# First attention of a two-layer block: probabilities scaled before their transposes instead of outputs after the value matmuls

## The chip, the cores and the metric
The kernel runs on one core of a Trainium2 chip, as one program. The metric is the device time in microseconds of a whole execution, the median of several. The profile is of one further execution; its times are counted from the start of its span.

## The reference
`x` is 8 x 256 x 1024 and the context `ctx_4096` 8 x 256 x 1024, both float32. Two layers of gated attention and feed-forward follow one another. Only the attention of layer 0 is touched here:

```python
x = rmsnorm(layernorm(x), ln_w)
q = (x @ wq.T)                       # 32 heads of 32
k, v = ctx @ wk.T, ctx @ wv.T        # 8 heads of 32, each used by 4 query heads
scores = q @ k.T / sqrt(32)          # 256 x 256 for each of 8 x 32 heads
attn = softmax(scores, axis=-1)
out = (attn @ v) ... @ wo.T
x = x + tanh(g_xattn[0]) * out
```

Softmax is exp(s - max) divided by its row sum. The division can be done on the probabilities or, since the sum belongs to a query row, on the rows of `attn @ v`.

## The kernel before
The program is a row of stages, each a block in which the five engines run their own instruction lists and meet only by semaphores: context projections, attention 0 (`attn0_stage`), its output projection, the feed-forward of layer 0, attention 1 and the last matmul. Attention 0 is the stage from about 178 to 684 us.

In it the 8 batches are taken two per turn of a loop (three turns, and the last pair written out). A batch has 16 units, n = 0 to 15. A unit is one tile t = n // 2 of four heads, and one half qb = n % 2 of the 256 query rows. Step n of TensorE's list does, in this order: the eight transposes of the probabilities of unit n (line 941, four heads by two halves kt of the keys, into the two banks of `psT`); the four score matmuls of unit n+2 (line 931, into `psS`); the sixteen value matmuls of unit n-1 (line 954, into `psO`); and a piece of the next batch's query projection (steps 0 to 3: four transposes of x, line 890; step 4, 7, 10, 13: 24 matmuls; the others 12, line 906). In the last batch that place is taken by small matmuls for an update table (line 981). Behind the values of the second half of a tile stand two transposes (line 960) that turn the spread reciprocals into the layout of the outputs.

Softmax of unit n+2 in step n: VectorE takes the negated maximum of four heads (line 1038), ScalarE computes four exponentials with their sums (line 1115) into `prob`, which has two buffers, n % 2. ScalarE's step n is first the eviction of `psT` for unit n (line 1132), then these exponentials. In odd steps from 5 VectorE evicts the first bank instead (line 1078).

VectorE's step n is a list in this order: a split of the query or of the transposed x into high and low parts (lines 1031, 1033, where step n has one); the eviction of line 1078 (odd n from 5); in odd steps the reciprocal of a tile's eight sums (line 1083); the maximum of n+2; in even steps `normalise_o` of the tile before (lines 1046 and 1048: evict the transposed reciprocals, then multiply the values by them). Steps 6 and 9 also have statistics for the batch after next, step 12 its normalisation, which waits for GpSimd's `rstd_of` (lines 622 to 634). GpSimd's list has one copy per tile that spreads eight reciprocals over 256 columns (line 860), and `rstd_of` after the copy of tile 5.

Results of four tiles are stored by SyncE's queue (line 797), which also loads `q_stack` (line 789), the keys, the values and x.

```python
BANK0_DVE = set(range(XFILLS + 1, UNITS, 2))
COPY_STEP = {f + 1: f for f in range(XFILLS)}
for t in range(KT - 1):
    COPY_STEP[XFILLS + 1 + 3 * (t // 2) + 2 * (t % 2)] = XFILLS + t
```

Of the kernel before, what the change touches and what calls it, by code (L numbers as in the profile page):

```python
# [16 lines left out]
F32 = mybir.dt.float32  # L17
# [4 lines left out]
ALU = mybir.AluOpType  # L22
# [4 lines left out]
P = 128  # L27
B, S, D = 8, 256, 1024
TT = S // P
KT = D // P  # L30
PAIRS = B // 2
HD0, NH0, NKV0 = 32, 32, 8
# [3 lines left out]
JH0 = P // HD0  # L36
# [7 lines left out]
HALF_N = 512  # L44
# [15 lines left out]
def hold(engine, sh):  # L60

    engine.sem_inc(sh.held, 1)
# [624 lines left out]
def attn0_stage(nc, sh, c, scratch, wq, rows, norm):  # L687
# [11 lines left out]
    ident = sh.ident  # L699
    UNITS = KT * TT  # L700
# [9 lines left out]
    with ExitStack() as es:  # L710
        def sb(name, shape, dt=F32):
            return es.enter_context(nc.sbuf_tensor("a_" + name, shape, dt))

        def sem(name):
            return es.enter_context(nc.semaphore("a_" + name))
# [8 lines left out]
        v0 = sb("v0", [P, 2, TT, KV0])  # L724
        prob = sb("prob", [P, 2, JH0, S])
        probT = sb("probT", [P, 2, TT, JH0, P])
        negmax = sb("negmax", [P, 2, JH0])
        sums = sb("sums", [P, 2, TT, JH0])
        recip_head = sb("recip_head", [P, 2, TT, JH0])
        recip = sb("recip", [P, 2, TT, JH0, HD0])  # L730
        recipT = sb("recipT", [P, S])
        oT = sb("oT", [P, KT, S])
        psS = es.enter_context(nc.psum_tensor("a_psS", [P, 4, HALF_N], F32))
        psT = es.enter_context(nc.psum_tensor("a_psT", [P, 2, HALF_N], F32))
        psO = es.enter_context(nc.psum_tensor("a_psO", [P, 2, S], F32))
        psQ = es.enter_context(nc.psum_tensor("a_psQ", [P, HALF_N], F32))
        coefs = sb("coefs", [P, NE, KT, RR])
        masks = sb("masks", [P, NE, KT, RR], U8)
# [12 lines left out]
        scores_full, max_ready, exp_done = sem("scores_full"), sem("max_ready"), sem("exp_done")  # L751
        psT_full = [sem(f"psT_full{p}") for p in range(2)]
        psT_copied = [sem(f"psT_copied{p}") for p in range(2)]
        head_ready, recip_ready = sem("head_ready"), sem("recip_ready")
        psO_full, recipT_ready = sem("psO_full"), sem("recipT_ready")
        o_ready = sem("o_ready")
        o_stored = [sem(f"o_stored{h}") for h in range(2)]
        coefs_loaded = sem("coefs_loaded")
# [93 lines left out]

        @block.gpsimd
        def _(pool):
            def spread_reciprocals(b, t):


                pool.wait_ge(head_ready, KT * b + t + 1)
                hold(pool, sh)
                nc.gpsimd.tensor_copy(recip[:, t % 2], recip_head[:, t % 2].unsqueeze(3).broadcast_to([P, TT, JH0, HD0])  # L860
                                      ).then_inc(recip_ready, 1)

            def body(i, final):
                for u in range(2):
                    b = 2 * i + u
                    for t in range(KT):
                        spread_reciprocals(b, t)
                        if t == 5 and not final:
                            norm.rstd_of(pool, b + 2, rms=True)

            with pool.Fori(0, PAIRS - 1) as i:
                body(i, False)
            body(PAIRS - 1, True)

        @block.tensor
        def _(pe):
# [57 lines left out]
                last.then_inc(scores_full, 1)  # L934

            def transposes(b, n):
                pe.wait_ge(exp_done, UNITS * b + n + 1)
                for kt in range(TT):
                    pe.wait_ge(psT_copied[kt], UNITS * b + n + 1)
                    for j in range(JH0):  # L940
                        last = nc.tensor.transpose(psT[:, kt, j * P:(j + 1) * P],  # L941
                                                   prob[:, n % 2, j, kt * P:(kt + 1) * P], ident[:, :])
                    last.then_inc(psT_full[kt], 1)

            def values(b, u, n):
                t, qb = n // TT, n % TT
                if qb == 0:
                    pe.wait_ge(o_ready, KT * b + t + 1)
                for kt in range(TT):
                    pe.wait_ge(psT_copied[kt], UNITS * b + n + 2)  # L950
                for kt in range(TT):
                    for j in range(JH0):
                        head = (t // REP0) * JH0 + j
                        nc.tensor.matmul(psO[j * HD0:(j + 1) * HD0, 0, qb * P:(qb + 1) * P],
                                         v0[:, u, kt, head * HD0:(head + 1) * HD0], probT[:, n % 2, kt, j, :],
                                         start=(kt == 0), stop=(kt == TT - 1))
                if qb == TT - 1:
                    pe.wait_ge(recip_ready, KT * b + t + 1)
                    for s in range(TT):
                        last = nc.tensor.transpose(psO[:, 1, s * P:(s + 1) * P],  # L960
                                                   recip[:, t % 2, s, :, :].rearrange("p j c -> p (j c)"), ident[:, :])
                    last.then_inc(psO_full, 1)

            for f in range(XFILLS):
# [49 lines left out]
        def _(dve):  # L1014
# [20 lines left out]
            def maximum(b, n):  # L1035
                dve.wait_ge(scores_full, UNITS * b + n + 1)
                bank = 2 * (n % 2)
                nc.vector.tensor_reduce(negmax[:, n % 2, :], psS[:, bank:bank + 2, :].rearrange("p a (j k) -> p (a j) k", k=S),  # L1038
                                        AX_X, ALU.max, negate=True).then_inc(max_ready, 1)

            def normalise_o(b, t):

                if t % QUAD == 0:
                    dve.wait_ge(o_stored[t // QUAD], 16 * JH0 * b + 1)
                dve.wait_ge(psO_full, KT * b + t + 1)
                nc.vector.tensor_copy(recipT[:, :], psO[:, 1, :]).then_inc(recipT_ready, 1)
                dve.wait_ge(recipT_ready, KT * b + t + 1)
                nc.vector.tensor_tensor(oT[:, t, :], psO[:, 0, :], recipT[:, :], ALU.mult).then_inc(o_ready, 1)


            for use in range(Q_USES - 1):
                split(0, use, True)
            maximum(0, 0)
            maximum(0, 1)
            dve.wait_ge(coefs_loaded, 16 * 4 * NE)
            nc.vector.tensor_tensor(coefs[:, :, :, :], coefs[:, :, :, :], masks[:, :, :, :], ALU.mult).then_inc(masked_done, 1)
            dve.wait_ge(masked_done, 1)
# [4 lines left out]
            def copy_update(quarter):  # L1062
                dve.wait_ge(update_full, quarter + 1)
                nc.vector.tensor_scalar(update[:, quarter * QUARTER:(quarter + 1) * QUARTER], psQ[0:RR, 0:QUARTER], 0.5, None, ALU.mult
                                        ).then_inc(update_copied, 1)

            def body(i, final):
                for u in range(2):
                    b = 2 * i + u
                    more = not (final and u == 1)  # L1070
                    for n in range(UNITS):
                        if n == 0:
                            split(b, Q_USES - 1)
                        elif n in COPY_STEP and more:
                            split(b + 1, COPY_STEP[n])
                        if n in BANK0_DVE:
                            dve.wait_ge(psT_full[0], UNITS * b + n + 1)
                            nc.vector.tensor_copy(probT[:, n % 2, 0, :, :],
                                                  psT[:, 0, :].rearrange("p (j q) -> p j q", j=JH0)).then_inc(psT_copied[0], 1)
                        if n % 2:  # L1080
                            t = n // 2
                            dve.wait_ge(exp_done, UNITS * b + n + 1)
                            nc.vector.reciprocal(recip_head[:, t % 2], sums[:, t % 2]).then_inc(head_ready, 1)  # L1083
                        if n + 2 < UNITS:
                            maximum(b, n + 2)
                        elif more:
                            maximum(b + 1, n + 2 - UNITS)
                        if n and n % 2 == 0:
                            normalise_o(b, n // 2 - 1)

                        if n == 6 and not final:
                            dve.wait_ge(x_loaded[u], 16 * i + 16)
                            norm.stats_of(x[:, u], 0)
                        if n == 9 and not final:
                            norm.moments_of(dve, b + 2, x[:, u], last_tile_only=True)
                        if n == 12 and not final:
                            norm.normalise(dve, b + 2, x[:, u], x[:, u], norm.STEPS_RMS)
                        if n > UPDATE_STEP and (n - UPDATE_STEP) % 3 == 0 and not more:
                            copy_update((n - UPDATE_STEP) // 3 - 1)
                    normalise_o(b, KT - 1)  # L1100
                    if not more:
                        copy_update(3)

# [1392 lines left out]
```

## Time and profile before

| | us |
|---|---|
| median of 3 executions | 1555.8 (1555.3 to 1561.07) |
| the profiled execution, its own time | 1561.66 |
| its span | 1559.9 |
| busy: TensorE, VectorE, ScalarE, GpSimd | 1411.1, 993.5, 761.7, 429.0 |
| attention 0: first and last transposes of probabilities | 182.2 and 680.9 |

In the rows below a line number is followed by the engine (PE TensorE, PEld its weight loads, DVE VectorE, ACT ScalarE, POOL GpSimd), the operation, what it writes and reads, and its shape. The `a_` names are those of attention 0. Times of single instructions are read to some 0.05 us, since their ends overlap with the next one's start.

### The profile page before, as it was taken

To read this page: it belongs to the slowest core of one execution; us is meant where nothing else is said; L and a number is where in the kernel's file an instruction comes from. 1 tells how busy PE (TensorE), PEld (TensorE's weight loads), DVE (VectorE), ACT (ScalarE), POOL (GpSimd) and SP (SyncE) were. 2 spreads that over 40 slices of the span, in tenths; PEclk is the share of its full clock that TensorE was granted. 3 is DMA by queue.
4 is the path that set the end of the run, shared out by engine and by line. 5 is a ranking of instruction groups with operands and counts; after the bars stand their busy time and mean duration, and the time that the engine had idled before them with its cause. 6 is when DMAs were issued, how large, how long until landed. Compare 5 with 4: busy or idle time off the path is not lost. (4 is left out here: it accounts for less than half of the span.)

```text
span 1559.9 us, 29677 instructions
## 1 busy us (share of the span) xinstructions
PE 1411.1 (90%) x10918; PEld 1142.4 (73%) x10926; DVE 993.5 (64%) x1578; ACT 761.7 (49%) x1911; POOL 429.0 (28%) x467
## 2 busy tenths in 40 slices
PE   7997799999999999879999939999959999999478
PEld 6997798888988889657787728888736666666244
DVE  4362377677666776543323227787547999998687
ACT  4320277677666776742212101221127777777387
POOL 0010000101101010000101003243348888888324
PEclk9998899999999999989999969999979999999889
DMA  6643555365553652844554342200032222221013
GB/s 234 215 166 82 91 136 144 82 143 119 133 130 83 154 130 70 217 151 157 189 177 147 121 162 82 81 15 26 1 81 69 68 62 61 61 61 42 1 80 137
DMA packets 134277, 169.98 MB, mean 109 GB/s; under 512 B 28933, under 2 KB 106565, under 8 KB 134166
## 3 DMA queue, kind: packets, MB, share of 16 engines
q1 hardware_dynamic: 134166, 168.41, 38.4%
q8 instruction: 80, 1.31, 0.4%
q14 instruction: 31, 0.25, 0.1%
HBM read 84.84 MB, written 33.19 MB: 76 GB/s over the span
## 5 line engine op out<-in xcount | busy, mean ns | idle before, releaser
L1115 ACT ACTIVATE a_prob<-a_psS,a_negmax 128x256 f32<-128x256 f32 x512 | 237.0, 485 | 158.8 <-DVE a_negmax L1038 158.5
L1038 DVE TENSOR_REDUCE a_negmax<-a_psS 128x4 f32<-128x1024 f32 x128 | 154.4, 1207 | 70.8 <-PE a_psS L931 68.7
L860 POOL COPY a_recip<-a_recip_head 128x256 f32<-128x256 f32 x64 | 25.6, 400 | 531.7 <-DVE a_recip_head L1083 531.7
L941 PE MATMUL a_psT<-ident,a_prob 128*128 128x128 f32 x1024 | 137.5, 278 | 14.4 <-issue 6.0
L906 PE MATMUL a_psQ<-a_xT_hi,wq_hi 128*128 128x256 f32 x456 | 135.5, 297 | 0.4
L941 PEld LDWEIGHTS a_psT<-ident,a_prob 128*128 128x128 f32 x1024 | 116.4, 143 | 23.5 <-issue 12.6
L1132 ACT COPY a_probT<-a_psT 128x512 f32<-128x512 f32 x208 | 115.8, 609 | 34.5 <-PE a_psT L941 33.5
L906 PE MATMUL a_psQ<-a_xT_lo,wq_hi 128*128 128x256 f32 x456 | 127.8, 280 | 0.0
L906 PE MATMUL a_psQ<-a_xT_hi,wq_lo 128*128 128x256 f32 x456 | 127.7, 280 | 0.0
L1115 ACT ACTIVATION_READ_ACCUMULATOR a_prob<-a_psS,a_negmax 128x1 f32 x512 | 110.3, 216 | 0.0
L1290 PE MATMUL p_psY<-p_w_hi,p_o_hi 128*128 128x512 f32 x256 | 103.7, 405 | 2.5 <-DVE p_o_lo L1318 2.5
L2143 ACT ACTIVATE b_prob<-b_prob 128x1024 f32<-128x1024 f32 x64 | 67.9, 1061 | 77.3 <-DVE b_prob L2017 77.3
L1525 PE MATMUL f_psY<-w_ffn_hi,f_xT_hi 128*128 128x512 f32 x256 | 102.9, 402 | 1.4 <-DVE f_xT_lo L1553 1.4
L1525 PE MATMUL f_psY<-w_ffn_lo,f_xT_hi 128*128 128x512 f32 x256 | 102.1, 399 | 0.0
L1525 PE MATMUL f_psY<-w_ffn_hi,f_xT_lo 128*128 128x512 f32 x256 | 102.0, 399 | 0.0
L1290 PE MATMUL p_psY<-p_w_lo,p_o_hi 128*128 128x512 f32 x256 | 100.3, 392 | 0.0
L1290 PE MATMUL p_psY<-p_w_hi,p_o_lo 128*128 128x512 f32 x256 | 100.3, 392 | 0.0
L1612 ACT CAST f_xT_hi<-f_psT 128x512 fp32r<-128x512 f32 x32 | 16.7, 599 | 170.1 <-PE f_psT L1507 170.1
L931 PE MATMUL a_psS<-a_k_stack,a_q_stack 128*128 128x256 f32 x512 | 93.4, 305 | 4.2 <-issue 3.0
L2011 DVE TENSOR_REDUCE b_maxes<-b_psS 128x16 f32<-128x1024 f32 x64 | 78.0, 1219 | 27.3 <-PE b_psS L1919 26.4
L906 PEld LDWEIGHTS a_psQ<-a_xT_hi,wq_hi 128*128 128x128 f32 x456 | 86.7, 190 | 9.1 <-issue 5.9
L906 PEld LDWEIGHTS a_psQ<-a_xT_hi,wq_lo 128*128 128x128 f32 x456 | 85.9, 188 | 0.0
(234 smaller groups left out, 3524.3 us busy)
## 6 DMA issues: line engine op xcount, KB each, us to landing
a_q_stack<-a_q_hi SPq DMA_DIRECT2D x128, 128.0 KB, 2.7
a_q_stack<-a_q_lo SPq DMA_DIRECT2D x128, 128.0 KB, 2.9
c_raw<-lay_ctxT SPq DMA_DIRECT2D x16, 512.0 KB, 4.9
rows<-in_x SPq DMA_DIRECT2D x8, 1024.0 KB, 5.8
scratch_o<-a_oT SPq DMA_DIRECT2D x64, 128.0 KB, 2.1
p_o_lo<-scratch_o SPq DMA_DIRECT2D x8, 1024.0 KB, 5.5
p_x<-in_x SPq DMA_DIRECT2D x8, 1024.0 KB, 7.6
scratch_x<-p_x SPq DMA_DIRECT2D x8, 1024.0 KB, 4.0
```

Of the source, the lines that this page charges most:

```text
L860: nc.gpsimd.tensor_copy(recip[:, t % 2], recip_head[:, t % 2].unsqueeze(3).broadcast_to([P, TT, JH0, HD0])).then_inc(recip_ready, 1)
L906: last = nc.tensor.matmul(bank[:, 0:S], w[:, kt, t * P:(t + 1) * P], a[:, kt, :], start=(kt == 0 and w is wq.hi and a is xT_hi), stop=(kt ...
L931: last = nc.tensor.matmul(psS[:, 2 * (n % 2) + j // 2, (j % 2) * S:(j % 2 + 1) * S], q_stack[:, t, j, qb * P:(qb + 1) * P], k_stack[:, u, ...
L941: last = nc.tensor.transpose(psT[:, kt, j * P:(j + 1) * P], prob[:, n % 2, j, kt * P:(kt + 1) * P], ident[:, :])
L1038: nc.vector.tensor_reduce(negmax[:, n % 2, :], psS[:, bank:bank + 2, :].rearrange("p a (j k) -> p (a j) k", k=S), AX_X, ALU.max, negate=Tr ...
L1115: last = nc.scalar.activation(prob[:, n % 2, j, :], psS[:, 2 * (n % 2) + j // 2, (j % 2) * S:(j % 2 + 1) * S], ACT.Exp, bias=negmax[:, n % ...
L1132: nc.scalar.copy(probT[:, n % 2, kt, :, :], psT[:, kt, :].rearrange("p (j q) -> p j q", j=JH0)).then_inc(psT_copied[kt], 1)
L1290: last = nc.tensor.matmul(psY[:, 2 * t + h, :], a[:, u, kt, t * P:(t + 1) * P], w[:, kt, h * HALF_N:(h + 1) * HALF_N], start=(kt == 0 and ...
L1525: last = nc.tensor.matmul(psY[:, 2 * t + h, :], a[:, u, kt, rows], w[:, kt, cols], start=(kt == 0 and a is xT_hi and w is w_ffn.hi), stop= ...
L1612: nc.scalar.copy(xT_hi[:, u, 2 * n:2 * n + 2, :].rearrange("p k n -> p (k n)"), psT[:, n, :]).then_inc(xhi_ready, 1)
L2011: nc.vector.tensor_reduce(maxes[:, n % 2, :], psS[:, n % 2, :].rearrange("p (h k) -> p h k", h=NH1), AX_X, ALU.max).then_inc(max_ready, 1)
L2143: nc.scalar.activation(prob[:, n % 2, :], prob[:, n % 2, :], ACT.Exp).then_inc(exp_done, 1)
```

## The change
`recip`, `recipT`, the transposes of line 960 and the copy of line 860 go. VectorE takes the reciprocal of one unit's four sums in each step, for unit n+1 in step n, ahead of the maximum. GpSimd multiplies the whole unit of `prob` (128 x 1024) by it, in place, and TensorE's transposes wait for that instead of for the exponentials. The outputs are evicted by a plain copy.

```diff
-            def spread_reciprocals(b, t):
-                pool.wait_ge(head_ready, KT * b + t + 1)
+            def scale_probabilities(b, n):
+                pool.wait_ge(head_ready, UNITS * b + n + 1)
                 hold(pool, sh)
-                nc.gpsimd.tensor_copy(recip[:, t % 2], recip_head[:, t % 2].unsqueeze(3).broadcast_to([P, TT, JH0, HD0])
-                                      ).then_inc(recip_ready, 1)
+                nc.gpsimd.tensor_tensor(prob[:, n % 2], prob[:, n % 2],
+                                        recip_head[:, n // TT % 2, n % TT].unsqueeze(2).broadcast_to([P, JH0, S]), ALU.mult
+                                        ).then_inc(prob_scaled, 1)
...
-                        spread_reciprocals(b, t)
+                        for qb in range(TT):
+                            scale_probabilities(b, TT * t + qb)
                         if t == 5 and not final:
                             norm.rstd_of(pool, b + 2, rms=True)
...
             def transposes(b, n):
-                pe.wait_ge(exp_done, UNITS * b + n + 1)
+                pe.wait_ge(prob_scaled, UNITS * b + n + 1)
...
                 if qb == TT - 1:
-                    pe.wait_ge(recip_ready, KT * b + t + 1)
-                    for s in range(TT):
-                        last = nc.tensor.transpose(psO[:, 1, s * P:(s + 1) * P],
-                                                   recip[:, t % 2, s, :, :].rearrange("p j c -> p (j c)"), ident[:, :])
                     last.then_inc(psO_full, 1)
...
-            def normalise_o(b, t):
+            def copy_o(b, t):
...
                 dve.wait_ge(psO_full, KT * b + t + 1)
-                nc.vector.tensor_copy(recipT[:, :], psO[:, 1, :]).then_inc(recipT_ready, 1)
-                dve.wait_ge(recipT_ready, KT * b + t + 1)
-                nc.vector.tensor_tensor(oT[:, t, :], psO[:, 0, :], recipT[:, :], ALU.mult).then_inc(o_ready, 1)
+                nc.vector.tensor_copy(oT[:, t, :], psO[:, 0:S]).then_inc(o_ready, 1)
+
+            def reciprocals(b, n):
+                dve.wait_ge(exp_done, UNITS * b + n + 1)
+                nc.vector.reciprocal(recip_head[:, n // TT % 2, n % TT], sums[:, n // TT % 2, n % TT]).then_inc(head_ready, 1)
...
             maximum(0, 0)
             maximum(0, 1)
+            reciprocals(0, 0)
...
-                        if n % 2:
-                            t = n // 2
-                            dve.wait_ge(exp_done, UNITS * b + n + 1)
-                            nc.vector.reciprocal(recip_head[:, t % 2], sums[:, t % 2]).then_inc(head_ready, 1)
+                        if n + 1 < UNITS:
+                            reciprocals(b, n + 1)
+                        elif more:
+                            reciprocals(b + 1, 0)
                         if n + 2 < UNITS:
                             maximum(b, n + 2)
```

## Rows read from the trace of the kernel before

**Rows 1.** The page, section 1: busy us, share of the span, instructions.
```profile
PE 1411.1 (90%) x10918; PEld 1142.4 (73%) x10926; DVE 993.5 (64%) x1578; ACT 761.7 (49%) x1911; POOL 429.0 (28%) x467
```
**Rows 2.** Busy time by stretch: length, engines, PE clock, DMA share, GB/s.
```profile
240.00:303.00 63.00, 61.96 (x690) 55.79 (x689) 45.47 (x79) 45.23 (x160) 5.62 (x15) 1.00 0.51 122
```
**Rows 3.** Waits in 178 to 625 us: total, times, longest.
```profile
PEld a_psT L941 <- ACT a_prob L1115: 6.5, 6, 3.0
```
**Rows 4.** Timeline of TensorE: start, length; starts of batches, one fifth unit, the last.
```profile
314.20 1.06 PE L941 MATMUL a_psT<-ident,a_prob 128*128 128x128 f32 x8 [3.01 <-issue]
...
325.18 1.06 PE L941 MATMUL a_psT<-ident,a_prob 128*128 128x128 f32 x8
...
375.18 1.04 PE L941 MATMUL a_psT<-ident,a_prob 128*128 128x128 f32 x8
...
439.46 1.94 PE L941 MATMUL a_psT<-ident,a_prob 128*128 128x128 f32 x8 [2.98 <-issue]
...
502.36 1.04 PE L941 MATMUL a_psT<-ident,a_prob 128*128 128x128 f32 x8
...
624.80 1.04 PE L941 MATMUL a_psT<-ident,a_prob 128*128 128x128 f32 x8
...
680.12 1.09 PE L941 MATMUL a_psT<-ident,a_prob 128*128 128x128 f32 x8
```
**Rows 5.** Timeline around one pair of reciprocal transposes.
```profile
304.87 0.44 PE L960 MATMUL a_psO<-ident,a_recip 128*128 128x128 f32 x2
...
305.06 0.36 PE L906 MATMUL a_psQ<-a_xT_hi,wq_hi 128*128 128x256 f32 x1
...
305.54 0.41 DVE L1046 COPY a_recipT<-a_psO 128x256 f32<-128x256 f32 x1
```
**Rows 6.** Timelines of VectorE, ScalarE and GpSimd: one unit's chain, then four reciprocals.
```profile
315.78 1.22 DVE L1038 TENSOR_REDUCE a_negmax<-a_psS 128x4 f32<-128x1024 f32 x1 [2.67 <-PE a_psS L931]
...
317.04 0.47 ACT L1115 ACTIVATE a_prob<-a_psS,a_negmax 128x256 f32<-128x256 f32 x1 [1.09 <-DVE a_negmax L1038]
...
318.75 0.21 ACT L1115 ACTIVATION_READ_ACCUMULATOR a_prob<-a_psS,a_negmax 128x1 f32 x1
...
318.24 0.19 DVE L1083 RECIPROCAL a_recip_head<-a_sums 128x8 f32<-128x8 f32 x1
...
318.60 0.40 POOL L860 COPY a_recip<-a_recip_head 128x256 f32<-128x256 f32 x1 [10.04 <-DVE a_recip_head L1083]
...
331.94 0.19 DVE L1083 RECIPROCAL a_recip_head<-a_sums 128x8 f32<-128x8 f32 x1
...
339.84 0.19 DVE L1083 RECIPROCAL a_recip_head<-a_sums 128x8 f32<-128x8 f32 x1
...
347.39 0.19 DVE L1083 RECIPROCAL a_recip_head<-a_sums 128x8 f32<-128x8 f32 x1
...
364.64 0.19 DVE L1083 RECIPROCAL a_recip_head<-a_sums 128x8 f32<-128x8 f32 x1
```
**Rows 7.** Timeline of GpSimd: the first and the last of the seven instructions of `rstd_of`.
```profile
357.12 0.22 POOL L622 TENSOR_SCALAR norm_tmp<-norm_moments 128x2 f32<-128x2 f32 x1
...
359.45 0.72 POOL L634 TENSOR_TENSOR norm_rstd<-norm_tmp,minus_half 128x2 f32<-128x2 f32 x1
```
**Rows 8.** Groups of GpSimd (busy, mean ns); then one line's min/median/max.
```profile
L1848 POOL TENSOR_TENSOR b_halves<-b_prob 128x512 f32<-128x512 f32 x64 | 82.9, 1296 | 6.5 <-ACT b_prob L2143 6.0
...
L860 POOL COPY a_recip<-a_recip_head 128x256 f32<-128x256 f32 x64 | 25.6, 400 | 531.7 <-DVE a_recip_head L1083 531.7
...
L1814 POOL TENSOR_TENSOR b_kbd<-b_group_mask,b_keys_lo 128x512 fp32r<-128x512 f32 x16 | 20.4, 1276 | 0.0
...
L1489 POOL TENSOR_TENSOR stream<-stream,f_bias x16: 2441/3008/3392, 943.3 to 1116.6; 128x1024 f32 x12, 128x1024 f32<-128x1024 f32 x4
```
**Rows 9.** Busy time by stretch, as rows 2: after a loop's jump, and with gaps.
```profile
439.00:441.00 2.00, 1.54 (x8) 1.57 (x9) 0.00 (x0) 0.42 (x1) 0.00 (x0) 0.50 0.83 210
...
630.00:634.00 4.00, 3.30 (x39) 2.78 (x39) 2.01 (x4) 4.00 (x15) 0.00 (x0) 1.00 1.04 280
```

## What the change is expected to do
> **What bounds the kernel now.** The page comes first: one core, a span of 1559.9 us, TensorE busy for 90% of it, VectorE 64%, GpSimd 28% [rows 1]. That share is a mean over stages, so the second view is the table of busy time by stretch. In the attention stage (units run from 182 to 684 us) a stretch of 63 us has TensorE busy for 61.96, VectorE 45.5, ScalarE 45.2 and GpSimd only 5.6 [rows 2]. TensorE is the bound there, and GpSimd is almost free; that much speaks for the change. The third view is the table of waits: over seven batches TensorE's weight loads wait for the exponentials only 6.5 us in all [rows 3]. So the softmax chain has slack, but this view does not say how much per unit. The fourth is the timeline, which does.
>
> I call t(n) the start of the transposes of unit n. On TensorE a batch of 16 units goes from t(0) = 314.20 to the next t(0) = 375.18, which is 60.98 us. The 17 starts, whose first, fifth and last stand in [rows 4], lie apart by 1.81, 3.58, 2.79, 2.80, 5.07, 3.54, 3.70, 4.95, 3.71, 3.53, 5.12, 3.53, 3.71, 4.98, 3.68 and 4.48 us, so the first four units take 10.98 together. Units are short at first because they carry four transposes of x and long later because they carry 12 or 24 matmuls of the next query.
>
> **What it removes.** Each second unit loses two transposes of the spread reciprocals: from their start at 304.87 to the next matmul at 305.06 is 0.19 us, and there are 64 such pairs [rows 5]. Worth 64 x 0.19 = 12 us where TensorE is the limit, nothing where it waits. VectorE loses an eviction of 0.41 us per tile [rows 5]; it has idle time in each unit, so I cost that at nothing. GpSimd loses 64 copies of 0.40 us, also nothing [rows 8].
>
> **What it adds, and where.** A reciprocal of 0.19 us on VectorE in each unit instead of each second (hidden by VectorE's idle 17 us in 63 [rows 2], apart from its place in the chain), and a two-input GpSimd multiply on 128x1024 between the exponentials and the transposes.
>
> **The price P of the multiply** is in no row of this stage. Nearest is the same shape in a later stage: 2.44 us at best, median 3.01; half that shape, 128x512, takes 1.296 on average beside a VectorE that mostly reads PSUM [rows 8], as it does here. Doubling 1.296 gives 2.6, but part of that is fixed. I take P = 2.5, next to the lowest whole-shape row, with ends of 1.0 (if a broadcast operand cost no reading; 128x256 with a broadcast copy takes 0.40 [rows 8], four times that is 1.6, less a fixed part) and 3.0 (the median, beside a VectorE on SBUF data). The Trainium skill (GPSIMD Engine Reference, section 3.1) puts a two-input elementwise operation at about 2.6 cycles per element at 1.2 GHz, which makes an estimate of 2.2 us here; by that the sum below would be about 18 us smaller. [...]
>
> **The chain over two units.** `prob` has two buffers, and the scores of unit n+2 are issued only after the transposes of n. Read off one unit [rows 4, 6]: transposes at 314.20, maximum starts 315.78 (1.58 later; I take 1.61, counted from the weight load), exponentials start 317.04 (1.26), last accumulator read ends 318.75 + 0.21 = 318.96 (1.92). New behind it: about 0.07 to the reciprocal, 0.36 from a reciprocal's start to GpSimd's (318.24 to 318.60), P, and 0.1 to TensorE; the two small gaps are estimates from the 0.04 to 0.1 that other hand-overs in these rows take. So t(n+2) is at least t(n) + 1.61 + 1.26 + 1.92 + 0.53 + P = t(n) + 5.3 + P, 7.8 us for a pair. Today the first two pairs take 10.98; they become 15.6.
>
> **The chain over one unit.** The reciprocal of unit n+1 now stands in VectorE's queue in step n, behind the split of the query and, in odd steps from 5, behind the eviction of psT, which waits for the transposes of n itself. Queued behind it is the maximum of n+2, for which ScalarE waits. From the reciprocal's start to TensorE is 0.36 + P + 0.1 = 2.96. Today's reciprocals in odd steps stand in that same place: step 5 at 331.94, 1.69 after its t; step 7 at 339.84, 2.35 after (two statistics are ahead of it); step 9 at 347.39, 1.24 after; step 13 at 364.64, 2.60 after (the row normalisation is ahead) [rows 6]; the four t, added up from the distances above, are 330.25, 337.49, 346.15 and 362.04. So these units take 4.65, 5.3, 4.2 and 5.55. Step 11 has another: the reciprocal square root follows scale 11 in GpSimd's queue, and runs from 357.12 to 359.45 + 0.72 = 360.17, 3.05 us [rows 7]; scale 12 is queued behind it: 3.05 + 2.5, less 0.1 of overlap with the start of step 11 and plus 0.1 to TensorE, is 5.55.
>
> **One batch**, in us, units in order: 0 to 3: 15.6; 4: 4.85; 5: 4.65; 6: 3.5; 7: 5.3; 8: 3.7; 9: 4.2; 10: 4.9; 11: 5.55; 12: 3.5; 13: 5.55; 14: 3.7; 15: 4.3. The units 4, 6, 10, 12 and 15 are TensorE's own time of today less 0.19. The sum is 69.3 against 60.98: 8.3 more. Seven batches have queries: 58. Less 3.5, since the seventh has no statistics and no rstd, and the fifth began at the slower clock and so was already longer: 62.90 from 439.46 to 502.36. The eighth has 55.3 us from its t(0) to its t(15) [rows 4]; seven pairs and a unit at the pair chain's 3.9 make 58.5, and the units with update matmuls stay above that in part: plus 4. The end loses an eviction of 0.41 and the pair of transposes: minus 0.5. Total plus 58. The loop's jump, about 3 us of TensorE every two batches, covers GpSimd's own jump and multiply (3 + 2.5), so nothing there.
>
> **Sum.** The profiled execution took 1561.66, which is 5.9 above the median of 1555.8. 1561.66 + 58 = 1620; against the median 1614. No DMA is moved; o and q transfers only get more time. About 0.5%, 8 us, is what a measurement of this kernel can tell from no change.
>
> **Rivals.**
> 1. *The multiply is cheap and hidden; not slower.* If P is near 1.0, a pair needs 6.3, the first four units 12.6 (1.6 more than today), every later unit goes back to TensorE's time, and seven removed pairs of transposes a batch give back 1.3. Net 0.3 a batch: 1558. For it: the second operand is one number per row. Against: of the two rows for 128x512, 1.276 has a broadcast operand (a mask repeated over a middle dimension) and 1.296 has none [rows 8]. Up to P = 1.5, one more us a batch, it would still not be told from no change; the gain would need P under about 0.9. Chance 0.07.
> 2. *Only the pair chain binds.* If splits and psT evictions run early enough, because TensorE is stalled and VectorE catches up, units 5 to 15 cost 7.8 per pair or their own time: 15.6 + 4.85 + 7.8 + 4.85 + 7.8 + 4.9 + 7.8 + 4.9 + 7.8 = 66.3, 5.3 a batch, plus 3 elsewhere: +40, 1596. Against: the odd-step eviction waits on t(n) whatever came before. Chance 0.18.
> 3. *Contention.* VectorE and GpSimd slow each other and P is 3.0. Eight steps of a batch hold P: 4 us a batch more, 32 in all: 1646. For it: the same shape ranges from 2.44 to 3.39 [rows 8]. Against: nearly all of VectorE's work here reads PSUM. The Trainium skill (GPSIMD Engine Reference, section 8) states contention only with VectorE instructions of two SBUF inputs or in a two-port mode; by that the rival stays small, and the trace agrees in that the 128x512 rows average 1.28 to 1.30. Chance 0.1.
> 4. *TensorE's clock falls.* In 439 to 441 us, just after 3 us of idle, the granted clock is 0.50 (1.2 GHz); in 630 to 634, with idle gaps of up to 2.1, it stays 1.00 (2.4 GHz) [rows 9]. The new gaps are under 2 us, except behind the loop's jump, where 2 us are added to 3. Today such a start cost the fifth batch 1.9 us (62.90 against 60.98). With a slow start in all batches, doubled by the further gaps: 8 x 3.8 = 30, 1644. Chance 0.1.
>
> **How the numbers follow.** The forecast has 0.55 and its own range of 1600 to 1630. The range reaches from under rival 2 and the smaller P (1588) to rivals 3 and 4 (1648). Faster 0.02 and same 0.05 come from rival 1 with P at its low end; slower is the rest, 0.93.
>
> **What would show it.** In the profile after: GpSimd busy in the stage some 128 x 2.5 = 320 us; TensorE's weight loads of the transposes waiting for GpSimd's write of `prob` by 80 us or more in all; a batch of 69 us, with 7.8 per pair in its first four units; scale 12 starting 3 us after scale 11 ended. Wrong if the multiply takes under 1.5 us, if TensorE still works through a batch in 61, or if the time after t(11) is that of unit 5.

## The result, and the profile after

The changed kernel takes 1579.6 us (median of 4) where the kernel before takes 1556.1 (median of 4). The medians lie 23.5 us apart; the recorded ratio of all fast runs is 1.0135, 95% interval 1.0115 to 1.0156, which is 21 us, and the text goes by the ratio. The forecast had the sign and the chain over two units, and more than twice the size: 1614, with a range that began at 1588.

First the page of the changed kernel, its busy times and the one row of GpSimd that is new (section 1; then the groups by line, columns as in [rows 8]), with what waited for it.

```profile
PE 1400.0 (89%) x10790; PEld 1128.0 (72%) x10798; DVE 979.3 (62%) x1578; ACT 761.0 (48%) x1911; POOL 645.8 (41%) x531
```
```profile
L856 POOL TENSOR_TENSOR a_prob<-a_prob,a_recip_head 128x1024 f32<-128x1024 f32 x128 | 242.4, 1893 | 333.9 <-DVE a_recip_head L1045 332.4 <-POOL norm_rstd L634 1.5
...
L939 PEld LDWEIGHTS a_psT<-ident,a_prob 128*128 128x128 f32 x1024 | 115.7, 144 | 66.0 <-POOL a_prob L856 55.2 <-issue 9.9
...
L1045 DVE RECIPROCAL a_recip_head<-a_sums 128x4 f32<-128x4 f32 x128 | 22.1, 172 | 61.2 <-ACT a_prob L1112 61.2
```

GpSimd is busy for 217 us more than in [rows 1], and the price P of the multiply is 1.893 us, with almost no spread. TensorE's weight loads of the transposes wait 55.2 us in all for it; in the kernel before they waited 6.5 us for the exponentials in a stretch of seven batches [rows 3]. The third row is a second wait that was not there: VectorE stands 61 us at the reciprocal, waiting for ScalarE, with the next maximum queued behind it.

The timeline of TensorE in the first units of the batch that begins at 387.22, which answers to [rows 4]:

```profile
387.22 1.09 PE L939 MATMUL a_psT<-ident,a_prob 128*128 128x128 f32 x8
...
390.78 1.09 PE L939 MATMUL a_psT<-ident,a_prob 128*128 128x128 f32 x8 [1.50 <-POOL a_prob L856]
...
394.35 1.09 PE L939 MATMUL a_psT<-ident,a_prob 128*128 128x128 f32 x8 [0.84 <-POOL a_prob L856]
...
397.91 1.09 PE L939 MATMUL a_psT<-ident,a_prob 128*128 128x128 f32 x8 [0.84 <-POOL a_prob L856]
...
401.47 1.09 PE L939 MATMUL a_psT<-ident,a_prob 128*128 128x128 f32 x8 [0.84 <-POOL a_prob L856]
```

The four units take 401.47 - 387.22 = 14.25 us, 7.13 a pair, where the forecast's formula 5.3 + P gives 7.2 for P = 1.89. From here on t(n) is read at the weight load of the first transpose, which moves single units by up to 0.1 us. The sixth batch, which has no loop jump in it, takes 63.67 us from t(0) to t(0), against 61.27 for the same batch before. Its units, in order: 3.56, 3.57, 3.56, 3.57, 4.82, 4.08, 3.47, 4.86, 3.50, 3.68, 4.82, 4.10, 3.46, 4.86, 3.50, 4.26. Units 0 to 3, 5, 9 and 11 are those in which the next transposes start right behind the multiply; the others are TensorE's own time and 0.09 to 0.3 shorter than before. The removed transposes account for most of that, not for all: units 7 and 13 had none.

Over the stage of the two profiled executions: t(0) of the first batch is 4.0 us later, the eight batches are 1.4, 2.5, 4.3, 2.6, 1.8, 2.4, 2.3 and 1.0 longer, and the end gives back 0.8: 21.4 us. Of the 4.0 the change made 2.3: from the first scores to t(0) 6.28 us pass instead of 3.98. The other 1.7 had passed before the first scores, where nothing of the change has run; over all twelve traces the first scores start anywhere from 178.2 to 180.9. So the stage itself costs 19.7 in this pair. The spans differ by 16.9 only, since 4.5 us less pass in the later stages of the changed kernel's execution; the profiled execution of the kernel before was itself 5.5 above its median.

### The profile page after: what moved, and what is told of

Same layout as the page of the kernel before. It is cut to its first block and busy times, and to the rows that moved or that the text cites. A ratio compares the mean times of both kernels' runs of the same rounds, so it can differ in the third digit from the quotient of the medians.

```text
span 1576.8 us, 29597 instructions
## 1 busy us (share of the span) xinstructions
PE 1400.0 (89%) x10790; PEld 1128.0 (72%) x10798; DVE 979.3 (62%) x1578; ACT 761.0 (48%) x1911; POOL 645.8 (41%) x531
## 5 line engine op out<-in xcount | busy, mean ns | idle before, releaser
L856 POOL TENSOR_TENSOR a_prob<-a_prob,a_recip_head 128x1024 f32<-128x1024 f32 x128 | 242.4, 1893 | 333.9 <-DVE a_recip_head L1045 332.4
L939 PEld LDWEIGHTS a_psT<-ident,a_prob 128*128 128x128 f32 x1024 | 115.7, 144 | 66.0 <-POOL a_prob L856 55.2
L1112 ACT ACTIVATION_READ_ACCUMULATOR a_prob<-a_psS,a_negmax 128x1 f32 x512 | 104.0, 203 | 0.0
L1360 POOL TENSOR_TENSOR w_ffn_lo<-p_full,w_ffn_hi 128x512 f32 x16 | 20.4, 1293 | 184.9 <-ACT w_ffn_hi L1397 184.9
```

The lines of the kernel that those rows point to most:

```text
L856: nc.gpsimd.tensor_tensor(prob[:, n % 2], prob[:, n % 2], recip_head[:, n // TT % 2, n % TT].unsqueeze(2).broadcast_to([P, JH0, S]), ALU.m ...
L939: last = nc.tensor.transpose(psT[:, kt, j * P:(j + 1) * P], prob[:, n % 2, j, kt * P:(kt + 1) * P], ident[:, :])
L1112: last = nc.scalar.activation(prob[:, n % 2, j, :], psS[:, 2 * (n % 2) + j // 2, (j % 2) * S:(j % 2 + 1) * S], ACT.Exp, bias=negmax[:, n % ...
```

## Experiments

Each is a small edit of the changed kernel or of the one named. Ratios are to the kernel before, run beside it on the same chip.

**1. The multiply nearly without its duration.** Only two of 256 columns of each head are scaled, so most of the normalisation is left out; every wait stays.

```diff
-nc.gpsimd.tensor_tensor(prob[:, n % 2], prob[:, n % 2],
+nc.gpsimd.tensor_tensor(prob[:, n % 2, :, 0:2], prob[:, n % 2, :, 0:2],
-    recip_head[...].unsqueeze(2).broadcast_to([P, JH0, S]), ALU.mult
+    recip_head[...].unsqueeze(2).broadcast_to([P, JH0, 2]), ALU.mult
```


> The changed kernel with the GpSimd multiply cut to 2 of the 256 key columns of each head (the other columns stay unscaled, so most of the normalisation is left out); every wait, the reciprocal of each unit and the plain eviction stay. Theory A (all of the 21 us comes from the multiply's duration P = 1.89 in the chain, and the removed transposes do pay): with P near 0.3 the pair chain is 5.5, the steps go back to TensorE's time, and the removed pairs of transposes are gained: 1546 to 1550. Rival B (the cost lies in VectorE's queue: the maximum now stands behind a reciprocal that waits for exponentials): still above 1560.

Measured 1549.4, ratio 0.9938 (0.9914 to 0.9962). The instruction takes 0.20 us. The rest of the change is worth 10 us, and the multiply's duration costs those and 21 more. Rival B falls as an account of the whole. It has a part, though: VectorE's timeline in the first units of the sixth batch of this run.

```profile
502.25 0.18 DVE L1045 RECIPROCAL a_recip_head<-a_sums 128x4 f32<-128x4 f32 x1 [0.68 <-ACT a_prob L1112]
502.34 1.23 DVE L1032 TENSOR_REDUCE a_negmax<-a_psS 128x4 f32<-128x1024 f32 x1
...
505.57 0.18 DVE L1045 RECIPROCAL a_recip_head<-a_sums 128x4 f32<-128x4 f32 x1 [0.68 <-ACT a_prob L1112]
```

The reciprocals are 3.32 us apart, and each waits for exponentials although the multiply costs next to nothing. That is a ring of its own: exponentials of n+1, 1.92, reciprocal and hand-overs 0.14, maximum of n+2 1.26, and then the exponentials of n+2. Units 2 and 3 take 3.33 each here and 2.80 before; the first four take 12.1 against 11.3. The forecast had the reciprocal's place in the queue, but not this ring.

Not all of the 10 us come from the removed transposes. The matmuls of the query start 0.118 us apart in the kernel before and 0.113 in the changed one, at the same granted clock and already ahead of the stage. These windows, of the kernel before and then of the changed one, count the matmuls of that line alone (length, TensorE, weight loads, clock, DMA share, GB/s).

```profile
160.00:174.00 14.00, 14.00 (x121) 14.00 (x120) 1.00 0.44 104
```
```profile
160.00:174.00 14.00, 14.00 (x125) 14.00 (x125) 1.00 0.33 79
```

Over the seven batches with queries the mean distance is 0.1168 before and 0.1143 in this run, which makes 3 us (an estimate, 1176 distances). Run 5 below has 0.118 ahead of the stage too, but so has run 9, and the other runs have 0.113: it goes neither with the multiply nor with the transposes, and its cause is open.

**2. A full operand.** The broadcast reciprocals are replaced by a tile of ones, so the normalisation is left out.

```diff
-nc.gpsimd.tensor_tensor(prob[:, n % 2], prob[:, n % 2],
-    recip_head[:, n // TT % 2, n % TT].unsqueeze(2).broadcast_to([P, JH0, S]), ALU.mult
+nc.gpsimd.tensor_tensor(prob[:, n % 2], prob[:, n % 2], unit[:, :, :], ALU.mult
```


> The changed kernel with the multiply by a full 128x1024 tile of ones in place of the broadcast reciprocals (the normalisation is left out). It asks where the forecast's P of 2.5 failed. Theory A1 (the broadcast of one number over 256 columns saves reading time): the multiply takes 2.44 to 2.5 and, by the forecast's chain with the rest as measured, a batch takes 67.9 instead of 63.7 and the whole 1610 to 1618. Rival A2 (two-input multiplies of this shape take 1.9 whatever the operand, and the 2.44 was contention): the multiply takes 1.9 and the time stays at 1579.

Measured 1606.1, ratio 1.0300 (1.0275 to 1.0326). This view is of the line's instructions, min/median/max in ns:

```profile
L858 POOL TENSOR_TENSOR a_prob<-a_prob,a_unit x128: 2340/2382/2407, 183.5 to 724.9; 128x1024 f32<-128x1024 f32 x128
```

The tile of ones is written once, ahead of the loop (not shown in the diff). A1 holds in kind: with a full second operand the same multiply takes 2.38 us, with one number for 256 columns 1.89. The time missed its expected 1610 to 1618 by 4 us; P is 2.38 and not 2.44 to 2.5, which at the price of the next sentence accounts for 3 to 6 us. Between these two kernels 0.49 us of P makes 26 us, 53 us per us.

**3. The multiply twice.** The probabilities are scaled by the squared reciprocal.

```diff
+nc.gpsimd.tensor_tensor(prob[:, n % 2], prob[:, n % 2], recip..., ALU.mult).then_inc(first_done, 1)
+pool.wait_ge(first_done, UNITS * b + n + 1)
 nc.gpsimd.tensor_tensor(prob[:, n % 2], prob[:, n % 2], recip..., ALU.mult).then_inc(prob_scaled, 1)
```


> The changed kernel with the multiply done twice in a row on the same unit, the second waiting for the first (the probabilities are scaled by the squared reciprocal). Theory A: P is 3.9 to 4.0, the first four units of a batch take 2 x (5.24 + 4.0) = 18.5 instead of 14.3, a batch about 80 to 84, the whole 1700 to 1750. Rival (GpSimd's part is mostly beside other work): below 1650.

Measured 1728.6, ratio 1.1101 (1.1067 to 1.1135): as theory A has it. The first four units of the sixth batch take 18.6 us, and a batch 82 to 86 (the last, without a query, 74). The rival, below 1650, falls.

```profile
607.39 0.86 PEld L944 LDWEIGHTS a_psT<-ident,a_prob 128*128 128x128 f32 x8 [1.55 <-POOL a_prob L861]
...
626.00 0.86 PEld L944 LDWEIGHTS a_psT<-ident,a_prob 128*128 128x128 f32 x8 [2.67 <-POOL a_prob L861]
```

The four kernels with P = 0.20, 1.89, 2.38 and 3.8 stand at -0.6%, +1.35%, +3.0% and +11.0%. One us of P costs 18 us on average between the first two, 53 and then 86: the more units of a batch are set by the multiply, the steeper. Between 0.20 and 1.89 nothing was run.

**4. Scores ahead of transposes.** If the pair chain holds the scores and the maximum because scores of n+2 stand behind the transposes of n in TensorE's list, then turning the two shortens it.

```diff
 for n in range(UNITS):
-    transposes(b, n)
+    pe.wait_ge(exp_done, UNITS * b + n + 1)
     if n + 2 < UNITS:
         scores(b, i, u, n + 2)
     elif more:
         scores(b + 1, i + u, 1 - u, n + 2 - UNITS)
+    transposes(b, n)
```


> The changed kernel with TensorE issuing the scores of unit n+2 ahead of the transposes of unit n, after a wait for the exponentials of n. Theory A: the pair chain no longer holds scores and maximum; what is left is exponentials 1.92, hand-over 0.43, multiply 1.89, 0.1, transposes and the eviction of their second bank about 1.7, which is 6.0; the first four units take about 12.1 instead of 14.3, the later steps stay as they are (VectorE's queue holds their reciprocals): about 1562, 1556 to 1568. Rival B (VectorE's queue sets the short steps): no change from 1579.

Measured 1561.3, ratio 1.0008 (0.9997 to 1.0020): nearly all of the 21 us gone, 18 by the medians and 20 by the ratios. Units 0 to 3 of the sixth batch take 3.08, 3.30, 3.32, 3.32, together 13.0 instead of 14.25. That is not the expected 12.1: what now ends last is the ring of experiment 1. The batch fell by more than its short units, 61.8 against 63.67, because unit 5 went from 4.08 to 3.64 and unit 11 from 4.10 to 3.90, which was not expected and is not explained here. So of 1.9 us a batch the pair chain accounts for the 1.2 of the first four units.

**5. The same order in the kernel before.**

```diff
-    transposes(b, n)
+    pe.wait_ge(exp_done, UNITS * b + n + 1)
     ...scores of n + 2...
+    transposes(b, n)
```


> The kernel before, with TensorE's scores of unit n+2 ahead of the transposes of unit n and nothing else. It asks whether the 18 us that this order took off the changed kernel belong to the multiply's chain. Theory A: here the steps are TensorE's own but for the first four of a batch, where at most 1.2 us lie above its work: 0 to 5 us faster, 1554 to 1560 against 1560. Rival: the order is worth the same 18 us anywhere (1542).

Ratio 0.9993 (0.9981 to 1.0006), 1559.0 against 1560.9. The order is worth nothing there that can be told, so the rival's 1542 falls: the 18 us are there only with the multiply in place.

**6. The reciprocal ahead of the eviction of psT**, on top of 4, in VectorE's odd steps from 5.

```diff
+    reciprocals(b, n + 1)        # in its three cases
     if n in BANK0_DVE:
         dve.wait_ge(psT_full[0], UNITS * b + n + 1)
         nc.vector.tensor_copy(probT[:, n % 2, 0, :, :], ...)
-    reciprocals(b, n + 1)
```


> scores_first with VectorE's reciprocal of unit n+1 ahead of its eviction of psT in the odd steps from 5. Theory (those steps wait for the multiply because the reciprocal stood behind an eviction that waits for this unit's transposes): steps 5, 9 and 11 go from 3.64, 3.64 and 3.90 to 3.50 to 3.55, 0.6 a batch: about 1557, 1555 to 1559. Rival: unchanged, 1561.

Ratio 0.9995 (0.9984 to 1.0006), 1560.1 against 1560.9. The time stays where the rival had it, and misses the expected 1555 to 1559. Units 5 and 9 do go to 3.49 as expected, so the place behind the eviction was what held them; at 0.15 each that is too little to tell in the whole. Unit 11 does not: it takes 3.97. GpSimd's timeline shows why.

```profile
421.24 0.22 POOL L622 TENSOR_SCALAR norm_tmp<-norm_moments 128x2 f32<-128x2 f32 x1
...
423.57 0.71 POOL L634 TENSOR_TENSOR norm_rstd<-norm_tmp,minus_half 128x2 f32<-128x2 f32 x1
424.53 1.90 POOL L856 TENSOR_TENSOR a_prob<-a_prob,a_recip_head 128x1024 f32<-128x1024 f32 x1 [0.26 <-POOL norm_rstd L634]
```

Here scale 12 waits for the end of `rstd_of`, which costs the unit half a microsecond (3.97 against 3.49).

**7. `rstd_of` two units later**, on top of 6, and the normalisation that needs it too.

```diff
-                        if t == 5 and not final:
+                        if t == 6 and not final:
                             norm.rstd_of(pool, b + 2, rms=True)
...
-                        if n == 12 and not final:
+                        if n == 14 and not final:
```


> recip_early with GpSimd's rstd_of moved from behind scale 11 to behind scale 13, and the normalisation that waits for it from step 12 to step 14 on VectorE. Theory: step 11 took 3.97 us against 3.49 for its neighbours because scale 12 stood behind 3 us of rstd_of; behind scale 13 the same 3 us lie beside the 4.85 us step 13: step 11 goes to 3.5, six batches, 3 us less: 1557 where the kernel before has 1560.9, a ratio of 0.997 to 0.999. Rival: it only moves the wait to step 13 or 14, ratio 0.9995 to 1.001.

Ratio 0.9982 (0.9968 to 0.9996), 1558.2 against 1560.4. Unit 11 takes 3.49 and unit 13 5.03 instead of 4.85. It came out as expected. Of the versions that keep the whole computation this is the only one whose interval lies under the kernel before, by 0.2%, and its end is 0.9996; that small gain is close to nothing. Against the changed kernel it is about 1.5% less.

**8. The maximum ahead of the reciprocal in the short steps**, on top of 6, to break the ring of experiment 1.

```diff
-                        reciprocals(b, n + 1)
+                        if n >= XFILLS:
+                            reciprocals(b, n + 1)
...
                         maximum(b, n + 2)
+                        if n < XFILLS:
+                            reciprocals(b, n + 1)
```


> recip_early, with the maximum ahead of the reciprocal in steps 0 to 3. Theory: the 3.3 us of a short step are a chain of its own, exponentials 1.92, reciprocal 0.14, maximum 1.26, since the maximum of n+2 stands behind the reciprocal of n+1 that waits for exponentials; with the order turned it goes, and the short steps fall to the 6.0 pair: 1 us a batch less, about 1549, 1547 to 1554, under both kernels. Rival: the later reciprocal gives it back, 1557.

The rival had the right direction and too small a size: 1573.8, ratio 1.0087 (1.0074 to 1.0101), where it said 1557. VectorE's timeline at the start of the fourth batch:

```profile
384.82 0.42 DVE L1028 TENSOR_TENSOR a_q_lo<-a_psQ,a_q_hi 128x256 fp32r<-128x256 f32 x1
385.16 1.21 DVE L1033 TENSOR_REDUCE a_negmax<-a_psS 128x4 f32<-128x1024 f32 x1
386.30 0.17 DVE L1046 RECIPROCAL a_recip_head<-a_sums 128x4 f32<-128x4 f32 x1
```

The exponentials of unit 1 were done at 384.6, so its reciprocal could have started at 385.16, when the split ended; it starts 1.14 later, behind a maximum, and the multiply and the transposes are late by as much. In the trace the first units of a batch take 4.2 and 4.6 at their longest. With the multiply in the chain the reciprocal is the more urgent of the two.

**9. The reciprocals on GpSimd**, on top of 7, so that VectorE's queue holds none.

```diff
-pool.wait_ge(head_ready, UNITS * b + n + 1)
+pool.wait_ge(exp_done, UNITS * b + n + 1)
+nc.gpsimd.tensor_tensor(recip_head[...], sums[...], unit[:, :], ALU.pow).then_inc(head_ready, 1)
+pool.wait_ge(head_ready, UNITS * b + n + 1)
```


> rstd_late with the reciprocals taken off VectorE: GpSimd raises the four sums to the power -1 itself, waits for it, and multiplies. It tells the two chains of a short step apart. If the 3.3 us of steps 1 to 3 are the chain over VectorE's queue (exponentials 1.92, reciprocal 0.14, maximum 1.26), they go although P grows by 0.8 to 1.1, and become the pair chain 6.0 - 0.36 + 0.9 = 6.5, or 3.25 a step, with odd and even steps unlike: no gain in sum, and the long steps stay at TensorE's time: ratio 0.998 to 1.001. If they were the pair chain over the multiply, they grow by 0.4 a step, 1.5 us a batch: ratio 1.004 to 1.01.

Ratio 1.0186 (1.0163 to 1.0209), outside both expectations. The power over 128x4 takes 1.01 us, so P is about 3.0 with the hand-over. The first four units take 14.0 against 13.0; the first expectation gives 13.0 and the second 14.6. Units 6, 12 and 13 grow too (4.25, 4.25, 6.25), which neither has. The run doesn't separate the two chains: both may have been at work in the kernel it was made from. Experiment 1 does, and the ring over VectorE rests on that.

**10. The multiply in two halves of the keys**, on the changed kernel alone.

```diff
+for kt in range(TT):
+    keys = slice(kt * P, (kt + 1) * P)
-    nc.gpsimd.tensor_tensor(prob[:, n % 2], prob[:, n % 2], ...
+    nc.gpsimd.tensor_tensor(prob[:, n % 2, :, keys], prob[:, n % 2, :, keys], ...
...
-                pe.wait_ge(prob_scaled, UNITS * b + n + 1)
                 for kt in range(TT):
+                    pe.wait_ge(prob_scaled, TT * (UNITS * b + n) + kt + 1)
```


> The changed kernel with the multiply in two instructions, by halves of the keys, each releasing its four transposes. Theory A: the half costs 1.0 to 1.05, so the second half ends 2.05 after the start and its four transposes 0.45 later, against 1.89 + 0.9: 0.3 a pair of units less, 8 a batch in the steps that wait: 1572 to 1578. Rival (a GpSimd instruction has a fixed cost that eats it): 1579 or more.

Measured 1573.4, ratio 1.0079 (1.0063 to 1.0094); a half takes 1.04 us, so both together 2.08 against 1.89.

```profile
L858 POOL TENSOR_TENSOR a_prob<-a_prob,a_recip_head x256: 1038/1040/1044, 183.1 to 693.2; 128x512 f32<-128x512 f32 x128
```

That is inside the expected 1572 to 1578. GpSimd is busy for longer and the kernel takes 6 us less than the changed one (9 by the ratios, whose intervals are apart): it is the latency to the transposes that counts, not GpSimd's load.

## Why the prediction was right in sign and wrong in size

- **What bounds the kernel, and that the multiply lands in a chain over two units: right.** 5.3 + P gives 7.2 a pair; 7.13 was measured. In runs 2 and 3 it gives 7.7 and 9.1, and the first pair of the sixth batch takes 7.6 and 9.1. Of the forecast's other signs, the size of each fell short with P: GpSimd's multiplies take 242 us and not 320, TensorE's weight loads wait 55 and not 80 or more, a batch takes 63.7 and not 69.
- **The step that failed is the price P**, "I take P = 2.5, next to the lowest whole-shape row". It is 1.893. The rows it came from all had two operands that change along the row; run 2 shows that this is the difference, 2.38 against 1.89. The mask with a broadcast over a middle dimension, 1.276 in [rows 8], was read as a sign that broadcasts save nothing. It repeats a row and not one number, which is another case. The copy of 128x256 at 0.40 from just such an operand was used for the lower end only. With P = 1.89 in the forecast's own table a batch comes to 65.2 instead of 69.3, and its sum to about +27 instead of +58. That is 1583, under the range too: the range began at 1588 although the forecast let P go down to 1.0.
- **Step 11: the wrong wait.** The forecast added the 3.05 us of `rstd_of` and a multiply from t(11) on, and named as a sign of being wrong that the unit takes as long as unit 5. It does: 4.10 against 4.08, where the table gives 4.94 at the right P. Scale 11 ends 1.09 us before t(11) = 562.20, since unit 10 is a long one of TensorE, so most of `rstd_of` lies in that time. What ends last is the reciprocal behind the eviction, as in unit 5; the rows are from the sixth batch, of VectorE and of GpSimd.

```profile
563.90 0.17 DVE L1045 RECIPROCAL a_recip_head<-a_sums 128x4 f32<-128x4 f32 x1
```
```profile
563.40 0.71 POOL L634 TENSOR_TENSOR norm_rstd<-norm_tmp,minus_half 128x2 f32<-128x2 f32 x1
564.36 1.89 POOL L856 TENSOR_TENSOR a_prob<-a_prob,a_recip_head 128x1024 f32<-128x1024 f32 x1 [0.25 <-POOL norm_rstd L634]
```

  Scale 12 starts 0.46 after its reciprocal, where other units have 0.35: `rstd_of` costs 0.1 here, and the half microsecond of run 6 only when the reciprocal comes earlier. Over six batches the step was 5 us too long.
- **What else stands between 27 and the stage's 19.7.** Units 8 and 14 kept 3.7 in the table, though they lose a pair of transposes as well (3.50 measured): 0.4 a batch too much. In the other direction the first batch was left out: the multiply also stands before its first transposes, 2.3 us that the forecast put at nothing. That the sum at the right P comes as near as 27 to 21 is in part luck of these terms.
- **A slip of counting.** By its own table seven multiplies a batch count, not the eight of rival 3, so its 32 us are 28, and the 18 us less by the Trainium skill's price are 16.
- **Steps 5, 9: right** (4.04 and 3.6 at that P, measured 4.08 and 3.68), and run 6 shows that the eviction ahead of the reciprocal was the reason. Steps 7 and 13, 4.7 and 4.95 by the chain, fell back to TensorE's 4.86.
- **Removed transposes: right in sign, the size not separated.** Run 1 is 10 us under the kernel before although it has the ring over VectorE, but some 3 us of that are the closer matmuls of the query. Units 7 and 13, which had no such transposes, are 0.09 and 0.14 shorter; units 4 and 10, as long and with a pair each, 0.26 and 0.29.
- **Missing from the forecast:** that ring, exponentials, reciprocal, maximum, 3.32 us a unit. It is hidden under the pair chain's 3.56 in the changed kernel, and is the next limit once that is shortened.
- **The loop's jump: nothing, as the forecast had it.** Unit 15 with the jump takes 7.54 and 7.51 us against 7.71 and 7.68 before. What differs is the start behind it: the third batch is 4.3 longer, where its neighbours are 2.5, and in it TensorE started at a granted clock of 0.50 (1.2 GHz) in the changed kernel's trace and of 1.00 (2.4 GHz) in the other's. These windows are of the two kernels, the first of the changed one: length, five busy times, and then the granted clock.

```profile
322.00:324.00 2.00, 1.97 (x10) 2.00 (x11) 0.00 (x0) 0.58 (x1) 0.43 (x1) 0.50 0.66 163
```
```profile
314.00:316.00 2.00, 1.80 (x16) 1.83 (x17) 0.22 (x1) 1.08 (x2) 0.00 (x0) 1.00 0.69 182
```

  The idle time before is 3.2 us in the changed kernel and 3.0 in the other, and the kernel before has such a slow start too, at 439 us, behind 3.0 us ([rows 4], [rows 9]). So one slow start more or less in a profile is not shown to be the change's doing. Rival 4 as a cost in each batch fell: in 387 to 454 us the clock is 1.00.
- **Rivals.** Rival 1 named 1.5 us as the point up to which nothing could be told; at 1.89 the cost is 21 us, and run 1 at 0.20 gives a gain of 10. No run stands between, so its own P of 1.0 was not tried. Rival 2 (only the pair chain) is closer in size than the forecast but not how it went: units 5, 9 and 11 are above TensorE's time. Rival 3 fell: the multiply's 128 times lie between 1.892 and 1.897.
- **The Trainium skill's price.** The measured 1.89 is under both prices in the forecast. The estimate of 2.2 us worked out from the Trainium skill (GPSIMD Engine Reference, section 3.1) lies between the 1.89 of the broadcast and the 2.38 of the full operand. It was nearer than my 2.5, by 0.3 against 0.6.

## What to carry to other kernels

An operation put into a producer-consumer chain costs its latency times the units in which that chain ends last, whatever the load of its engine: list the units one by one with what sets each, and put the new duration into that list. Before paying for it, look at what the in-order lists put into the chain for no reason; here the order of two groups of matmuls was worth 18 of the 21 us with the multiply in place, and nothing that can be told without it. A price read from rows of the same shape must also match in how each operand is read.

## What the runs showed of the hardware

- GpSimd's two-input multiply on 128x1024 float32 takes 1.893 us when the second operand is one number per 256 columns and 2.38 us when it is a full tile; 128x512 with the broadcast takes 1.040, 128x8 0.203. From 512 to 1024 columns it adds 0.85 us.
- It hardly varies here (1.892 to 1.897) beside a VectorE that is busy for some two thirds of the time; the full operand varies from 2.340 to 2.407.
- GpSimd's power over 128x4 takes 1.007 us, five times its multiply on 128x8.
- TensorE's matmuls of 128x256 with a weight load each start 0.118 us apart in three of the twelve programs and 0.113 in the other nine, at granted clock 1.00 and in a stretch whose instructions are the same in all. No run shows why.
